# Two mixture-of-experts routers and a unit norm run inside the layer norm's block, the picking of routed tokens takes eight highest at a time, and an expert's bias is added on VectorE

## The chip, the cores and the metric

The kernel runs as one program on one core of a Trainium2 chip. The metric is the device time of one execution in microseconds. All data are fp32. An fp32 product of two 128x128 tiles, or a transpose of one, shows in the trace as one or two matmul instructions on TensorE (PE), each with a weight load (PEld) of its own: a transpose or a product with a 0/1 matrix takes one, a product of two full fp32 tiles two.

## The reference

Eight blocks run one after the other on x, 4096 tokens (16 rows of 256) by 128, each as `x = layernorm(x + block(x))`. Four of them matter here.

- **L0's FFN** is a mixture of 8 experts. `logits = x @ router_w + router_b`; the two highest of each token get the softmax of the two as their gates; the output is the gated sum of the two experts.
- **L1's FFN** is a mixture of 8 experts with bias. The scores are `softmax(x @ gate_w.T + gate_b)`; of the two highest of a token only the expert with the higher number is used (as the kernel computes it, `win`), with its score as the gate. Its output is `gelu(xs @ w1 + b1) @ w2 + b2` of the scaled token `xs`.
- **L2's FFN** has a light attention over all tokens and a heavy one over routed tokens:

```
def rmsnorm(x, gamma):
    norm = jnp.maximum(jnp.linalg.norm(x, axis=-1, keepdims=True), 1e-12)
    return x / norm * x.shape[-1] ** 0.5 * gamma
def route(x, routing_token, num_tokens):
    s = jnp.einsum('bnd,d->bn', x, routing_token)
    scores = coor_descent(s, k)                        # 50 iterations
    sel_scores, sel_idx = jax.lax.top_k(scores, num_tokens)
    return (sel_scores + stop_gradient(1.0 - sel_scores), sel_idx)
...
light_out = light_local_attn(x, gamma_light, wq_light, wkv_light, wo_light)
scores_q, idx_q = route(x, q_routing_token, NQ)        # 128 of the 256 of a row
scores_kv, idx_kv = route(x, kv_routing_token, NKV)    # all 256
heavy_out = zeros.at[b, idx_q].set(heavy_attn(...) * scores_q)
return light_out + heavy_out
```

- **Every layer norm** is applied at the start of the next block: a block ends with x + block(x) in `X` and each token's mean and variance in `core.mv`.

## The kernel before

`X` holds the tokens, 32 tiles of 128 tokens (partitions) by 128; `XT` holds them transposed, 128 by 4096. A group is 4 tiles, 512 tokens, and fills one of the 8 PSUM banks. The program is a row of Blocks. Within one, each engine runs its own instructions in the order in which they are written, and waits on semaphores; no scheduler moves anything. Between two Blocks all engines meet at a barrier, and SyncE (SP) then gives each new semaphore one credit, for which the first instructions wait.

**normalize_stage** (L296, L313, L323, L302). VectorE (DVE) makes 1/std and writes the 32 normalized tiles, PE transposes 8 groups of 4 into 8 banks, ScalarE (ACT) copies groups 0 to 4 to `XT`, and DVE, done with its own, groups 5 to 7.

**gate_stage** (L1412 to L1447), a Block of its own behind a norm, in two places (names g_...). PE forms the logits with the router's weights as the stationary operand, 8 rows by 512 tokens at a time; ACT copies them to `g_LT`; 32 small transposes (L1416) turn them by token. DVE adds the bias, and for each of the 32 tiles takes MAX8 and FIND_INDEX8 (L1454, L1458). L0 then turns the gates back by expert with 32 transposes (L1427) and 8 copies by ACT to `f_gatesT`, which the FFN's Block stores to DRAM (L1555) and loads spread over the partitions (L1561, `f_spread`); DVE multiplies by it at L1628. L1 has a third Block, **l1_places** (names p_..., L1740 to L1776), that counts the tokens of each expert before each token (`f_place`) and the expert of each of the 40 sorted tiles (`f_expert`).

**l1_ffn.** POOL scatters the 32 tiles of tokens to `x_sorted` (L1872), SP loads them back in order of expert (L1857, `f_xin`), and a loop written out over 40 sorted tiles (slots) follows. In a slot PE transposes the scaled tile n (L1899), forms the hidden rows of n-1 (L1906) and the output of n-2 (first the bias as a row of ones by `f_b`, L1914, then four products, L1917). DVE scales tile n (L1972), and adds, normalizes and takes the moments of older tiles (L1975 to L1990). POOL copies the next expert's `w1` to `f_w` and scatters finished tiles. PE, ACT and POOL each read the number of the expert into a register (L1839).

**l2_ffn.** normalize_stage; routing_start (the scores of the two routing tokens, 16 matmuls of 32 rows, and the scaling of six weights by gamma on DVE); normalize_stage once more as unit norm (names nu_...; squares and sums on DVE, then `normed`, L294); the light attention, `wide_stage` "5l", in which the 50 iterations of the descent are interleaved; routing_finish (L3316 to L3368), which ranks each token among the 256 of its row by comparing it with all of them, two rows at a time; the heavy attention, "5h", which takes the tokens whose rank is below 128, in the order of their rank.

Of the kernel before, what the change touches and what calls it, by code (L numbers as in the profile page):

```python
# [23 lines left out]
ALU = mybir.AluOpType  # L24
# [13 lines left out]
W_COLS = (5760, 8864)  # L38
# [29 lines left out]
def shape_constants():  # L68
# [16 lines left out]
    before = np.concatenate([(c < q), (c < q + P)], 1).astype(np.float32)  # L85
# [10 lines left out]
        ("bucket", onehot), ("future", neg), ("logk", logk), ("before", before),  # L96
        ("order", np.tile(np.arange(P, dtype=np.float32), (P, 1))),
        ("iota8", np.tile(np.arange(8, dtype=np.float32), (P, 1))),
    ]
# [12 lines left out]
STAGED = {"rope32q": 0, "ones": 0, "rope32k": 0, "rope8q": 2, "rope8k": 2, "bucket": 2, "future": 2, "before": 5, "order": 5}  # L112
# [26 lines left out]
def place_weights(items, region_cols):  # L139

    at, out = 0, {}
    for name, rows, cols in items:
# [15 lines left out]
        ("l1_lower", 128, 128), ("l1_ones", 128, 128), ("l1_multiples", 128, 32), ("l1_earlier", 128, 64),  # L158
# [3 lines left out]
        ("l2_tok", 128, 64), ("before", 128, 512), ("order", 128, 128),  # L162
# [66 lines left out]
def normalize_stage(core, ctx, n, first=False, unit=None, into=None, beside=None, next_weights=()):  # L229
# [5 lines left out]
    SQUARES = 8  # L235
    LOADS = 4 if first else 0
    BY_ACT = 5
    credited = []
    sem = lambda s: new_sem(core, ctx, f"n{n}_{s}", credited)
    with ExitStack() as mem:  # L240
        mem.callback(retire, core, credited)
        std = mem.enter_context(nc.sbuf_tensor(f"n{n}_std", [P, TILES], F32))
        sq = mem.enter_context(nc.sbuf_tensor(f"n{n}_sq", [P, SQUARES, DM], F32)) if unit is not None else None
        normed = X if unit is None and into is None else unit if into is None else into
        x_loaded = [sem(f"x_loaded{k}") for k in range(LOADS)]
        var_ready, std_ready, rstd_ready = sem("var_ready"), sem("std_ready"), sem("rstd_ready")
        group_normed, group_turned, squared = sem("group_normed"), sem("group_turned"), sem("squared")
        ident = core.const("ident")
        block = mem.enter_context(nc.Block())

        @block.sync
        def _(sp):
# [9 lines left out]
            if beside:  # L262
                beside(sp)

        @block.vector
        def _(dve):
# [3 lines left out]
            elif unit is not None:  # L270
                squared_so_far = counter(CREDIT)
                for c in range(0, TILES, SQUARES):
                    dve.tensor_tensor(sq[:, :, :], X[:, c:c + SQUARES, :], X[:, c:c + SQUARES, :], ALU.mult
                                      ).then_inc(squared, 1)
                    dve.wait_ge(squared, squared_so_far())
                    dve.tensor_reduce(core.rstd[:, c:c + SQUARES], sq[:, :, :], AX.X, ALU.add).then_inc(squared, 1)
                    dve.wait_ge(squared, squared_so_far())
# [1103 lines left out]


def gate_stage(core, ctx, n, w, m, dve_part, act_part, outs, setup=None):


    nc = core.nc
    credited = []
# [2156 lines left out]
```

## Time and profile before

| | |
|---|---|
| median of 3 runs | 2970.11 us (2969.63 to 2972.64) |
| profiled execution | 2968.71 us |
| its span | 2966.9 us |
| PE busy | 2421.8 us (82%) |
| weight loads (PEld) busy | 1869.1 us (63%) |
| DVE busy | 1951.4 us (66%) |
| ACT busy | 1396.2 us (47%) |
| POOL busy | 1397.5 us (47%) |
| mean granted TensorE clock | 0.932 of full |

The span runs from the first to the last instruction of the profiled execution; 1.8 us of its time lie outside. The shares are means over a program whose stages have different limits, so a stretch has to be read by itself. The granted clock is 1.0 at 2.4 GHz and 0.50 at 1.2 GHz.

### The profile page before, as it was taken

The numbers are of one execution on the slowest core, as the hardware profiler recorded it, in microseconds if no ns is written. First come the engines' busy times: TensorE is split into PE (matmuls) and PEld (weight loads), VectorE is DVE, ScalarE is ACT, GpSimd is POOL, SyncE is SP. The second block draws the span as 40 slices with busy tenths as digits, with TensorE's granted clock in tenths as the row PEclk, the third lists the DMA queues.
The fourth block names the chain that finished last, engine by engine and source line by source line (L and its number), as shares of the span: only waits on it lengthen the run. The fifth ranks groups of instructions, "written<-read, shape, count | busy, mean of one in ns | idle before, by whom it ended". The sixth has DMA issues, their size and how long they took to land. (4 is left out here: it accounts for less than half of the span.)

```text
span 2966.9 us, 73365 instructions
## 1 busy us (share of the span) xinstructions
PE 2421.8 (82%) x21662; PEld 1869.1 (63%) x21662; DVE 1951.4 (66%) x8496; ACT 1396.2 (47%) x3314; POOL 1397.5 (47%) x1606
## 2 busy tenths in 40 slices
PE   5888888779588872778998778956897899999977
PEld 4666666536366650666777567745776777777755
DVE  3666666646488873337888679975555676777746
ACT  1333333322366651445666446623554666656624
POOL 2666666400266652547777345632331444455401
PEclk7999999989799995889999989978999999999978
DMA  2000000022200001130000100000000000000001
GB/s 68 2 1 0 0 0 0 19 59 57 90 2 0 0 24 41 52 94 2 0 0 0 37 1 1 0 0 1 2 0 21 2 1 0 0 0 0 0 1 29
DMA packets 38235, 45.06 MB, mean 15 GB/s; under 512 B 6265, under 2 KB 28658, under 8 KB 37750
## 3 DMA queue, kind: packets, MB, share of 16 engines
q1 hardware_dynamic: 35774, 38.43, 4.6%
q0 software_dynamic: 2304, 4.79, 0.5%
q8 instruction: 68, 1.11, 0.2%
q14 instruction: 89, 0.73, 0.1%
HBM read 36.17 MB, written 9.74 MB: 15 GB/s over the span
## 5 line engine op out<-in xcount | busy, mean ns | idle before, releaser
L1081 POOL TENSOR_TENSOR a_sm<-a_sm,a_top 128x512 f32<-128x512 f32 x512 | 523.4, 1040 | 308.0 <-DVE a_top L879 306.0
L1004 ACT ACTIVATE a_pr<-a_sm 128x512 f32<-128x512 f32 x512 | 315.1, 626 | 236.5 <-POOL a_sm L1081 132.5
L879 DVE CUSTOM_DVE_ANT_0 a_sm<-bank,cst 128x256 f32<-128x256 f32 (+1 forms) x1024 | 300.9, 352 | 120.0 <-PE bank L741 120.0
L755 PE MATMUL bank<-cst,a_pr 128*128 128x128 f32 x2304 | 307.2, 277 | 0.6 <-ACT a_pt L1014 0.5
L2921 POOL TENSOR_TENSOR a_pr<-a_sm,a_rden 128x512 f32<-128x512 f32 x192 | 197.1, 1047 | 225.9 <-DVE a_rden L2707 225.4
L755 PEld LDWEIGHTS bank<-cst,a_pr 128*128 128x128 f32 x2304 | 259.6, 142 | 27.8 <-issue 20.4
L887 DVE COPY a_pt<-bank 128x512 f32<-128x512 f32 x272 | 187.0, 688 | 129.4 <-PE bank L755 125.0
L1014 ACT ACTIVATE a_pt<-bank 128x512 f32<-128x512 f32 x304 | 177.1, 588 | 98.2 <-PE bank L755 94.3
L2681 DVE CUSTOM_DVE_ANT_0 a_sm<-bank,cst 128x256 f32<-128x256 f32 (+1 forms) x512 | 149.7, 353 | 51.0 <-PE bank L2568 43.5
L775 PEld LDWEIGHTS bank<-a_pt,a_v 128*32 128x32 f32 x4608 | 118.3, 110 | 88.6 <-issue 77.8
L879 DVE CUSTOM_DVE_ANT_0 a_sm<-bank,a_bias 128x256 f32<-128x256 f32 (+1 forms) x512 | 148.4, 353 | 33.0 <-PE bank L741 30.0
L775 PE MATMUL bank<-a_pt,a_v 128*32 128x128 f32 x4608 | 155.9, 276 | 7.4 <-DVE a_pt L887 3.8
L2997 PE MATMUL bank<-a_xs,W 128*128 128x256 f32 x544 | 140.2, 392 | 17.8 <-ACT a_q L3010 10.7
L2921 POOL TENSOR_TENSOR a5h_pr<-a5h_sm,a5h_rden 128x512 f32<-128x512 f32 x64 | 65.6, 1046 | 158.3 <-DVE a5h_rden L2707 158.3
L1071 POOL COPY a_xs<-XT 128x256 f32 (+1 forms) x54 | 21.4, 399 | 225.7 <-SPq L619 225.7
L2827 ACT ACTIVATE a_sm<-a_sm,a_top 128x256 f32<-128x256 f32 x256 | 127.1, 505 | 0.0
L879 DVE DVE_READ_ACCUMULATOR2_ANT a_top<- 128x1 f32 x1536 | 126.9, 83 | 0.0
L2997 PEld LDWEIGHTS bank<-a_xs,W 128*128 128x128 f32 x544 | 95.8, 192 | 41.3 <-ACT a_q L3010 17.6
L741 PE MATMUL bank<-a_kx,a_q 32*128 32x512 f32 (+1 forms) x896 | 111.2, 579 | 9.0 <-POOL a_kx L1162 4.6
L1019 ACT ACTIVATE a_osb<-bank 128x256 f32<-128x256 f32 (+1 forms) x96 | 43.7, 455 | 158.9 <-PE bank L775 158.9
L2568 PE MATMUL bank<-a_k,a_q 64*128 64x256 f32 (+1 forms) x1024 | 96.8, 333 | 17.7 <-ACT a_k L3010 9.3
L805 PE MATMUL bank<-cst,a_rx 128*128 128x128 f32 x256 | 48.2, 290 | 76.6 <-DVE a_top L879 74.3
(484 smaller groups left out, 6156.6 us busy)
## 6 DMA issues: line engine op xcount, KB each, us to landing
f_spread<-gate_rows SPq DMA_DIRECT2D x16, 512.0 KB, 6.8
W<-in_l_w SPq DMA_DIRECT2D x2, 2048.0 KB, 9.7
x_sorted<-in_l_blank SPq DMA_DIRECT2D x4, 660.0 KB
f_xin<-x_sorted SPq DMA_DIRECT2D x10, 264.0 KB, 2.9
X<-in_x SPq DMA_DIRECT2D x4, 512.0 KB, 6.8
a_bias<-bias_rows SPq DMA_DIRECT2D x1, 2048.0 KB, 7.9
X<-y_rows SPq DMA_DIRECT2D x8, 256.0 KB, 5.5
out_x<-X SPq DMA_DIRECT2D x8, 256.0 KB, 2.3
```

Of the source, the lines that this page charges most:

```text
L741: mm = pe.matmul(sbank[j][:, col:col + m * kw], B["q"][b][r0:r0 + rows, c, qt * P:(qt + 1) * P], B["kx"][b][r0:r0 + rows, x:x + m, 0:kw], ...
L755: mm = pe.transpose(tbank[j % 2][:, c * P:(c + 1) * P], pr[j][:, c * P:(c + 1) * P], ident)
L775: mm = pe.matmul(O[32 * group:32 * group + 32, blk * P:(blk + 1) * P], B["v"][b][:, kb, hd.slot[h], :], pt[j][:, col:col + P], start=(kb = ...
L879: ins = dve.tensor_tensor_reduce(sm[j][:, m * kw:(m + 1) * kw], sbank[j][:, m * kw:(m + 1) * kw], mk, 1.0, 3.0e38, ALU.add, ALU.min, top[: ...
L887: dve.tensor_copy(pt[j][:, :], tbank[j % 2][:, :]).then_inc(S[f"turned_out{j}"], 1)
L1004: act.activation(pr[j][:, :], sm[j][:, :], ACT.Exp, scale=-1.0).then_inc(S["probs"], 1)
L1014: act.activation(pt[j][:, :], tbank[j % 2][:, :], ACT.Copy).then_inc(S[f"turned_out{j}"], 1)
L1081: pool.tensor_tensor(whole, whole, top[:, qt, a:a + m].unsqueeze(2).to_broadcast([P, m, kw]), ALU.subtract).then_inc(S["shifted"], 1)
L2681: ins = dve.tensor_tensor_reduce(sm[s % 2 * 4 + j][:, m * kw:(m + 1) * kw], sbank[j][:, m * kw:(m + 1) * kw], mk, 1.0, 3.0e38, ALU.add, AL ...
L2827: ins = act.activation(part, part, ACT.Exp, bias=top[:, s % 2, j, m:m + 1], scale=-1.0, accum_out=den[:, s % 2, j, m:m + 1])
L2921: pool.tensor_tensor(pr[j][:, :].rearrange("p (h k) -> p h k", k=kw), sm[q % 2 * 4 + j][:, :].rearrange("p (h k) -> p h k", k=kw), rden[:, ...
L2997: mm = pe.matmul(bank[:, c * SEQ:(c + 1) * SEQ], w[:, a:a + P], xs[:, :], start=True, stop=True)
```

## The change

**Norm and routers.** normalize_stage loses its unit form and takes `follow`, an object with a part for each engine that runs in the same Block. ACT now copies all 8 groups in every normalize_stage (before 5). With `follow`, PE forms the logits by token, with a tile of `XT` as the stationary operand and the router's 8 columns as the moving one. L0Gates and L1Gates replace gate_stage, top_entries and l1_places. They hold everything as 8 experts by 32 tiles (256 elements a partition); a reduction over experts reads elements 32 apart (`by_token`). The two highest are found by a maximum, a comparison, a product with 8..1 to take the first of equals, and another maximum. The sums before a tile come from one scan. The gates of L0 leave as two 128x128 transposes; their store is issued in this Block, and the spread loads wait for the first to land before the second is issued. In L1 POOL issues the 32 scatters in this Block.

```
+            def logits(g):
+                pe.wait_ge(copied, g + 1 + CREDIT)
+                for t in range(g * G, g * G + G):
+                    mm = pe.matmul(core.bank[0][:, 8 * t:8 * t + 8], XT[:, t * P:(t + 1) * P], follow.w, start=True, stop=True)
             for g in range(GROUPS):
...
                 for t in range(G):
                     mm = pe.transpose(core.bank[g][:, t * P:(t + 1) * P], normed[:, g * G + t, 0:DM], ident)
+                if follow and g >= 2:
+                    logits(g - 2)
...
+    def first_at(self, dve, values, highest, out):
...
+        self.then(dve, dve.tensor_tensor(self.eq[:, :, :], values[:, :, :], over(highest[:, :], SHE, 1), ALU.is_equal))
+        self.then(dve, dve.tensor_tensor(self.eq[:, :, :], self.eq[:, :, :], over(self.core.const("down8"), SHE, 2), ALU.mult))
+        self.then(dve, dve.tensor_reduce(self.c[:, :], by_token(self.eq), AX.X, ALU.max))
+        self.then(dve, dve.tensor_tensor(out[:, :, :], self.eq[:, :, :], over(self.c[:, :], SHE, 1), ALU.is_equal))
...
+    def dve(self, dve):
+        dve.wait_ge(self.logits_mm, 1 + CREDIT)
+        self.then(dve, dve.tensor_tensor(self.lg[:, :, :], self.logits, over(self.b, SHE, 2), ALU.add))
+        self.then(dve, dve.tensor_reduce(self.m[:, :], by_token(self.lg), AX.X, ALU.max))
+        self.first_at(dve, self.lg, self.m, self.one)
+        self.then(dve, dve.scalar_tensor_tensor(self.rest[:, :, :], self.one[:, :, :], -BIG, self.lg[:, :, :], ALU.mult, ALU.add))
+        self.then(dve, dve.tensor_reduce(self.r[:, :], by_token(self.rest), AX.X, ALU.max))
+        dve.tensor_tensor(self.a[:, :], self.r[:, :], self.m[:, :], ALU.subtract).then_inc(self.to_exp, 1)
+        self.first_at(dve, self.rest, self.r, self.two)
...
```

On PE, in the Block of the norm that stands before L0's FFN and the Block after it, before the change:

```order
L313 MATMUL bank<-cst,X 128x128 x32
L240 UNCONDITIONAL_BRANCH
L1407 UNCONDITIONAL_BRANCH
L1412 MATMUL bank<-XT,W 8x512 x8
L1416 MATMUL bank<-cst,g_LT 128x8 x32
L1427 MATMUL bank<-cst,f_gates 8x128 x32
L1393 UNCONDITIONAL_BRANCH
```

and after it, in one Block, where L309 is the transpose and L299 the router's product by token:

```order
L309 MATMUL bank<-cst,X 128x128 x12
L299 MATMUL bank<-W,XT 128x8 x4
L309 MATMUL bank<-cst,X 128x128 x4
L299 MATMUL bank<-W,XT 128x8 x4
L309 MATMUL bank<-cst,X 128x128 x4
...
L299 MATMUL bank<-W,XT 128x8 x12
L1479 MATMUL bank<-cst,n_gates 128x128 x2
L239 UNCONDITIONAL_BRANCH
```

The products now stand between the transposes, one group of 4 behind each from the third, and the last three groups of 4 behind the last transpose; the 64 small transposes are 2 large ones.

**Bias of an expert.** `f_b` becomes 128x1024, loaded from 4 KB of DRAM to all partitions (512 KB), and DVE waits for it before its first tile. DVE adds it.

```
-                        pe.matmul(y, w("l1_ones")[0:1, :], b2[:, bass.ds(e * DM, DM)], start=True, stop=False)
...
+                    for n in behind(3):
+                        e = expert(dve, n)
+                        dve.wait_ge(down, n + 1 + CREDIT)
+                        dve.tensor_tensor(yb[n % 2][:, :], YB[n % 2][:, 0:DM], b2[:, bass.ds(e * DM, DM)], ALU.add
+                                          ).then_inc(biased, 1)
```

On DVE, in the last slot of the ramp, where the first reciprocal stands, before:

```order
L1972 TENSOR_SCALAR f_xg<-f_xin 128x128
L1975 RECIPROCAL f_rstd<-f_std 128x1
L1978 TENSOR_TENSOR f_z<-bank,f_xin 128x128
L1984 TENSOR_SCALAR f_yout<-f_z,f_mv,f_rstd 128x128
L1988 BN_STATS f_stat<-f_z 128x6
L1990 BN_AGGR f_mv<-f_stat 128x2
```

and after (L1777 reads the expert's number into a register):

```order
L1903 TENSOR_SCALAR f_xg<-f_xin 128x128
L1777 TENSOR_LOAD f_expert
L1777 ISA x2
L1907 ISA
L1907 TENSOR_TENSOR f_yb<-bank,f_b 128x128
L1911 RECIPROCAL f_rstd<-f_std 128x1
L1914 TENSOR_TENSOR f_z<-f_yb,f_xin 128x128
```

The read of the bank moved ahead of the reciprocal, with a register load ahead of it; PE waits for this read instead of for L1978.

**Unit norm.** normalize 5, routing_start and the unit norm become one Block. The unit-length tile is written from the raw `X` as (X - mean)·scale, where scale comes from the variance that is already there; `X` itself is not normalized, and the light attention's end adds unit·length. PE transposes and forms the two routing products by tile, as in a router, ACT copies the even groups (after scaling three light weights) and DVE the odd ones.

**Picking.** routing_finish loses its loop; all 32 rows of 256 scores are handled at once:

```
+            for k in range(PICKS):
+                here = sc if k == 0 else left[(k - 1) % 2]
+                dve.max(eight[k % 2][:, :], here[:, :]).then_inc(found, 1)
+                dve.wait_ge(found, k + 1 + CREDIT)
+                dve.match_replace(left[k % 2][:, :], eight[k % 2][:, :], here[:, :], -1.0).then_inc(taken, 1)
+                dve.wait_ge(taken, k + 1 + CREDIT)
```

A scan over the tokens that were replaced gives each its place; two transposes bring it by token. The heavy weights are scaled here by ACT. On DVE, one iteration's first and last operations before:

```order
L3344 ISA r_prod,r_own<-bank,cst 128x128
L3344 ISA r_own 128x1
L3351 SCALAR_TENSOR_TENSOR r_tie<-bank,r_own,W 128x256 x4
L3357 SCALAR_TENSOR_TENSOR r_ahead<-bank,r_own,r_tie 128x256 x4
L3363 ISA
L3363 TENSOR_REDUCE rank<-r_ahead 128x2
```

and the whole of the picking's end after, behind 14 more pairs like the first two rows:

```order
L3351 MAX r_eight<-r_left 32x8
L3353 MATCH_REPLACE r_left<-r_eight,r_left 32x256
L3355 TENSOR_SCALAR r_picked<-r_left 32x256
L3358 SCALAR_TENSOR_TENSOR r_place<-r_ones,r_picked 32x256
L3360 SCALAR_TENSOR_TENSOR r_row<-r_place,r_picked 32x256
L3362 TENSOR_SCALAR rank<-bank 128x32
L3366 TENSOR_SCALAR r_chosen<-rank 128x32
L3369 TENSOR_TENSOR SQ<-SQ,r_chosen 128x32
```

A chain that handled 2 of 16 rows in each of 8 iterations is a chain of 16 pairs over all rows, each waiting for the one ahead.

## Rows read from the trace of the kernel before

**Rows 1.** Busy time by stretch: us, PE, PEld, DVE, ACT, POOL, clock, DMA, GB/s

```profile
27.00:50.00 23.00, 15.29 (x64) 14.25 (x64) 10.74 (x48) 1.28 (x1) 6.21 (x18) 0.50 0.00 0
1206.50:1210.00 3.50, 3.50 (x16) 3.05 (x15) 0.00 (x0) 2.45 (x9) 1.23 (x2) 0.50 0.00 0
1214.00:1300.00 86.00, 85.83 (x653) 77.44 (x652) 40.10 (x211) 55.63 (x206) 53.58 (x68) 1.00 0.17 48
```

**Rows 2.** Timeline, first router: start, us, engine, line, output<-inputs, [idle before <-releaser]

```profile
581.74 4.67 PE L313 MATMUL bank<-cst,X 128*128 128x128 f32 x20 [5.44 <-DVE X L296]
582.68 0.71 PEld L313 LDWEIGHTS bank<-cst,X 128*128 128x128 f32 x4 [0.25 <-DVE X L296]
585.75 0.42 PEld L313 LDWEIGHTS bank<-cst,X 128*128 128x128 f32 x4 [0.31 <-DVE X L296]
...
613.53 0.42 DVE L1516 TENSOR_TENSOR g_two<-g_two,g_p 128x256 f32<-128x256 f32 x1
613.99 0.42 DVE L1518 TENSOR_TENSOR f_gates<-g_one,g_two 128x256 f32<-128x256 f32 x1
...
622.73 0.36 SPq L1555 DMA_DIRECT2D gate_rows<-f_gatesT  x1
...
635.93 0.69 DVE L1628 TENSOR_TENSOR f_hid<-f_prod,f_spread 128x512 f32<-128x512 f32 x1 [6.93 <-DMA f_spread<-gate_rows]
```

**Rows 3.** Timeline of weight loads in the first attention's stage

```profile
33.49 1.78 PEld L478 LDWEIGHTS bank<-W,kv_xs 128*128 128x128 f32 x8 [0.92 <-DVE KV L489]
```

**Rows 4.** Single lines: ns min/median/max, first and last start, forms

```profile
L276 DVE TENSOR_REDUCE rstd<-nu_sq x4: 1219/1220/1220, 1703.7 to 1711.3; 128x8 f32<-128x1024 f32 x4
L2324 DVE TENSOR_REDUCE f_S<-f_ec x1: 1873/1873/1873, 2915.3 to 2915.3; 128x128 f32<-128x1024 f32 x1
L1454 DVE MAX8 g_vals<-g_lg x32: 150/151/170, 604.0 to 606.1; 128x8 f32<-128x8 f32 x32
```

**Rows 5.** Timeline, second router and the scatter by expert

```profile
1109.12 5.84 PE L313 MATMUL bank<-cst,f_moved 128*128 128x128 f32 x24 [5.44 <-DVE f_moved L296]
...
1158.65 1.17 POOL L1872 DMA_INDIRECT x_sorted<-f_moved,f_place  x1 [12.85 <-SPq L204]
...
1198.00 0.96 POOL L1872 DMA_INDIRECT x_sorted<-f_moved,f_place  x1 [0.31 <-issue]
...
1203.22 0.29 DVE L1972 TENSOR_SCALAR f_xg<-f_xin 128x128 f32<-128x128 f32 x1 [44.73 <-DMA f_xin<-x_sorted]
```

**Rows 6.** The page: DMA issues, KB each, median us from issue to landing

```profile
f_xin<-x_sorted SPq DMA_DIRECT2D x10, 264.0 KB, 2.9
X<-in_x SPq DMA_DIRECT2D x4, 512.0 KB, 6.8
```

**Rows 7.** Timeline of one slot of the expert loop

```profile
1228.69 0.48 PE L1914 MATMUL bank<-f_b,W 1*128 x2
...
1229.11 0.97 PEld L1917 LDWEIGHTS bank<-W,f_hT 128*128 128x128 f32 x8
...
1230.26 0.16 DVE L1975 RECIPROCAL f_rstd<-f_std 128x1 f32<-128x1 f32 x1 [1.31 <-ACT f_std L1953]
...
1231.20 0.48 PE L1914 MATMUL bank<-f_b,W 1*128 x2
```

**Rows 8.** The register load of an expert's number on ACT

```profile
L1839 ACTq TENSOR_LOAD <-f_expert x40: 272/278/491, 1204.4 to 1304.5; - x40
```

**Rows 9.** Timeline, start of L2's FFN and of its light attention

```profile
1683.32 5.70 PE L313 MATMUL bank<-cst,X 128*128 128x128 f32 x24 [5.44 <-DVE X L296]
...
1719.87 1.88 DVE L302 COPY XT<-bank 128x512 f32<-128x512 f32 x3
...
1724.51 0.74 POOL L2904 COPY a5l_xs<-XT 128x256 f32<-128x256 f32 x2 [49.33 <-SPq L2448]
```

**Rows 10.** Timeline of the picking

```profile
1965.91 0.41 ACT L3316 ACTIVATE r_sc<-d_t 32x256 f32<-32x256 f32 x1 [4.60 <-DVE d_t L3327]
...
2019.05 0.19 DVE L3368 TENSOR_TENSOR SQ<-SQ,r_chosen 128x32 f32<-128x32 f32 x1
```

## What the change is forecast to do

> **What bounds the kernel now.** The page gives PE 82% of the span, but the change touches stretches in which PE does little or nothing, so I read the busy time by stretch first. In the steady part of the expert loop PE is busy for 85.83 of 86 us at full clock [rows 1]: there an operation taken from PE shortens the slot, until another engine needs as long. Before it DVE waited 44.73 us for the scattered tiles [rows 5], while POOL scatters and nothing else has anything to do. Then the timelines. Around each router one operation hands to the next: 54.2 us lie between the first transpose (581.74) and the first product with the spread gates (635.93), which waited 6.93 us for a transfer [rows 2]; 49.5 us between the transpose at 1109.12 and the first scatter at 1158.65 [rows 5]. Before the light attention 41.2 us pass from the first transpose, at 1683.32, to 1724.51, when POOL begins its first copy [rows 9]. The picking holds PE and POOL up from the exponential at 1965.91 to 2019.24 (2019.05 + 0.19) [rows 10]. In these four stretches everything is on the path, so each microsecond counts whole.
>
> **Two prices that all of them need.** A DVE operation on 128x256 with a wait for the one before starts 0.46 us after it (613.53 to 613.99, of which 0.42 is the operation) [rows 2]. A maximum or sum over strided elements costs more: 1024 contiguous elements took 1.220 us, 1024 strided ones 1.873 [rows 4], 0.64 ns an element, 0.16 us for 256. The second price is TensorE's. Four transposes of a group load for 0.71 us at half clock and 0.42 at full [rows 2]. The four router products of a group are full fp32 products with a tile as the stationary operand, 8 weight loads; such 8 loads took 1.78 us at half clock [rows 3] and 0.97 at full [rows 7].
>
> **Norm with router.** DVE delivers a group each 1.03 us, and PE turns the first three as now, until 2.7 us after its start t. Then 5 groups of transposes and 8 of products are due: 5·0.71 + 8·1.78 = 17.8 us at half clock, 5·0.42 + 8·0.97 = 9.9 at full. PE becomes what this block waits for, and the granted clock decides. Now the clock rises 4.0 us after t in the first norm (581.74 to 585.75) [rows 2]. But in the attention's stage of 27 to 50 us the clock stays 0.50 with PE busy 15.29 of 23 us, and in the expert loop, PE busy throughout, it is still 0.50 at 1206.5 to 1210 and full by 1214 [rows 1], 3.3 to 10.8 us behind the first tile at 1203.22 [rows 5]. Between 4.0 and 10.8 I take the middle, 7.4. By then 4.7 us of the 17.8 are done; the rest at full clock takes 9.9·(1 - 4.7/17.8) = 7.3, and the logits stand at t + 14.7. The bounds are t + 13.2 (rise at 4.0) and t + 20.5 (no rise).
>
> **A, L0's router.** t = 581.74, logits at 596.4. DVE then runs 15 steps of 256 elements at 0.46 us, four of them strided at 0.16 more, and five small ones, the wait for ACT among them, some 1.1 us: 8.7. Two transposes and one copy of 128x256 on ACT take about 1.2. So the store is issued at 606.3 rather than 622.73. Store and load took 13.2 us (to 635.93) [rows 2]; the four loads then shared the queue. Now the first pair goes alone: a store of some 3 us, and 6.8, what a transfer of 512 KB needs to land [rows 6], 10.0 with the wait. The barrier, 1.4 us before, is hidden behind it. First gated product at 616.4 instead of 635.93: **19.5 us**.
>
> **B, L1's router.** t = 1109.12, logits at 1123.8. Up to `placed` DVE has some 31 steps of about 256 elements, 9 strided, and small ones between, with two waits (exponential, counts): 18.9 us, most of it 30·0.46 + 9·0.16 = 15.2 and the rest at small prices. POOL, in the same block, scatters at 1142.9 instead of 1158.65, no barrier standing between: 15.8 less. The 32 scatters keep their pace of (1198.00 - 1158.65)/31 = 1.27 us [rows 5]. Behind them something is given back. Now 4.3 us pass from the last scatter's end (1198.96) to the first tile at 1203.22. The barrier now lies behind the scatters (2.3 us with the credit), and SP's first transfer there is the spread `f_b`, 512 KB, for which DVE waits before its first tile, with the read of the scattered tiles behind it on the queue. I take 5.5 us for both, between 2.9 (the tiles alone, 264 KB) and the 6.8 of 512 KB [rows 6]. 2.3 + 0.4 + 5.5 = 8.2 against 4.3, 3.9 back: 15.8 - 3.9 = **11.9 us**.
>
> **C, bias on DVE.** PE's slot is 2.51 us (1228.69 to 1231.20). From L1914 to the first load of L1917 are 0.42 us [rows 7]; without it, 40 slots save 40·0.41 = **16.4 us**, to a slot of 2.09. The lower bound is the operation's own least share, 0.25 us a slot: 10. Does another engine need more? DVE is busy 40.10 us in 34.4 slots [rows 1], 1.17 a slot; the new addition (0.27) and the register load make it 1.9. The load takes 0.28 us where ACT does it [rows 8], with some 0.17 of register work. ACT: 55.63/34.4 = 1.62, and its own load 0.45: 2.07, the same as PE's, so it is full too. DVE now waits 1.31 us for ACT in each slot [rows 7]; the load falls into that wait. But `biased` comes later than the product ends by 0.6, and the next `f_xg` behind it by 1.2, and PE wants it 2.09 behind: 0.3 to spare. The Trainium skill (DMA: Bandwidth & Descriptors, Latency and other measured facts) puts a floor of about 600 ns on a register load, by which ACT's slot would be 2.39 and the gain some 5 us in place of 16.4. The trace has 0.28 and decides.
>
> **D, unit norm's block.** Before the first tile DVE and ACT have one more root, product, maximum, reciprocal and product, 1.3 us: t = 1683.32 + 1.3 = 1684.6, logits at 1699.4, of the same shape as a router's. Product with the length, two transposes, copy and maximum add 1.6: 1701.0. The work that stands there now ends at 1719.87 + 1.88 = 1721.75 [rows 9]; the way on to POOL's copy stays: **20.8 us**. Squares, sums (4·1.22 [rows 4]), the second norm and two barriers are gone. The scaling of weights goes to ACT, ahead of its first copy, 3·0.6 us beside DVE's first groups; if it delays the first copies, PE has transposes to do.
>
> **E, picking.** No instruction of the trace reads 256 elements in MAX8; with 8 it took 0.15 [rows 4]. At a sum's 1.05 ns an element, 248 more make 0.41. The replacement is two instructions, a load of 8 (0.09) and a pass like any of 256 elements, 0.42. With two waits a pair takes 1.00 us. It could be 0.8 if the two overlap, or 2.0 if each pass takes twice the time. 16 pairs are 16.0 us, and the tail (mark, scan, product, two transposes, three short steps) 2.5. The exponential ends 0.4 us sooner, at 1965.9, since the memsets are POOL's. So 1984.4 against 2019.24: **34.8 us** [rows 10]. The roots `sel`, the weights' scaling and the memsets run on POOL and ACT beside it, 3 us in all under 16.
>
> **F, the copies.** In the norms 2, 6 and 7 the last three copies, 1.88 us on DVE [rows 9], are ACT's now and end 0.4 us sooner each: **1.1 us**.
>
> **Sum.** 19.5 + 11.9 + 16.4 + 20.8 + 34.8 + 1.1 = 104.5. The profiled execution took 2968.71 us, so 2864.2; the median of the runs, 1.4 above it, gives 2865.6, rounded 2865.
>
> **Weighed against the skill.** The row says that strided reduction costs 0.64 ns more an element; 13 such reductions in A and B are 2.1 us, already in the sum. The Trainium skill (Advanced Engine Details and Errata, SBUF Cachelines) speaks against this layout, elements 32 apart in fp32: each access on another line of 16 bytes pays a penalty. The trace agrees and gives the penalty a size that the pages leave out.
>
> **The rivals.**
> - *The clock never rises in the three blocks.* For it speaks the stage of 27 to 50 us [rows 1], in which PE works with gaps; against it that with a backlog PE has no gaps here. Three times 20.5 - 14.7 = 5.8: 17.4 us less, 2883.
> - *The expert loop doesn't follow PE.* DVE's chain behind `down` has 0.3 us to spare, ACT's sum is level with PE's. If the slot stays at 2.51, 16.4 are lost: 2882. At 2.3, half.
> - *Picking at 2.0 us a pair*: 16 us less, 2881. Nothing in the rows speaks for it but the absence of such an instruction.
> - *Slower.* The register load on DVE: each slot it stands ahead of the read of the bank, and PE, ACT and POOL wait behind that. The other terms give 88.1 us; spread on 40 slots, 2.2 us. The kernel is slower by 6 us from a slot of 2.51 + 94/40 = 4.86, which needs a load of 3.4 us where ACT's takes 0.28. At a load of 3.5, the slot is 4.96 and the time 2970 - 88 + 98 = 2980.
> - *The change does not do what it says*: the longest of the stretches stays because another transfer ends it. For L0 the bound is the store and load, which I count in full; in the others no transfer stands at the end [rows 9, 10].
>
> **How the numbers follow.** I give my forecast 0.70, no rise of the clock 0.12, the loop 0.08, the picking 0.06, slower 0.02, no change 0.02. Downwards the clock's rise at 4.0 us gives 4.5, `f_b` with the tiles in 2.9 us gives 2.6, pairs of 0.8 us 3.2: together 10, and 5 for prices taken too high: 2850. Upwards each of the three rivals alone ends at 2881 to 2883; two at once and the last two cases are left out. So 2850 to 2884. Faster by over 0.2% (6 us, about what a measurement of this kernel tells from no change) holds in all cases but the last two: 0.97; within it 0.01; slower 0.02.
>
> **What would show it.** In the profile of the changed kernel: logits of the first router ended 14.7 us behind the first transpose, with eight loads at 0.97 in the second half of that time; the store at 606; the first scatter at 1142.9 and the first tile 8.2 us behind the last scatter's end; a slot of 2.09 with PE still busy all of it; POOL's copy into the light attention 19.1 us behind the block's first transpose (now 41.2); 16 pairs of 1.00 us. The sum is wrong if PE idles in the slot, if loads stay at 1.78 in the blocks, or if a pair of the picking shows over 1.2 us.

## The result, and the profile after

The changed kernel takes 2898.11 us (median of 4 runs, 2896.35 to 2898.73). The kernel before took 2971.32 beside it (4 runs, 2969.63 to 2972.64). The ratio is 0.9756, 95% interval 0.9744 to 0.9767: 73 us less, where 105 were forecast, and the time lies above the range's 2884. A correction: the section on the reference says that L1's experts use a gelu; they use a relu. No number rests on it.

| profiled execution | before | after |
|---|---|---|
| its time | 2968.71 us | 2898.5 us |
| its span | 2966.9 us | 2896.7 us |
| PE / DVE busy | 2421.8 / 1951.4 us | 2390.4 / 1916.4 us |
| ACT / POOL busy | 1396.2 / 1397.5 us | 1391.7 / 1391.9 us |
| mean granted clock | 0.932 | 0.932 |

The sums of busy time moved by 31 and 35 us for the two large engines and by 5 for the others, and say little; the stretches say it. Between the same two instructions of each stage:

| term | from, to | before | after | gain | forecast |
|---|---|---|---|---|---|
| A, L0's router | end of the attention before, to the first gated product | 58.5 | 46.0 | 12.5 | 19.5 |
| B, L1's router | first transpose to first tile | 94.1 | 90.6 | 3.5 | 11.9 |
| C, expert loop | first tile to L2's attention | 129.9 | 119.4 | 10.5 | 16.4 |
| D, unit norm | first DVE step of the norm to POOL's copy | 44.1 | 29.6 | 14.5 | 20.8 |
| E, picking | exponential to the last mark | 53.3 | 18.4 | 35.0 | 34.8 |

Together 76.0. The span fell by 70.2; the other 5.8 went the wrong way outside these five stretches, most of it in stages whose instructions the change does not touch (below).

The first router in the timeline of the changed kernel (start, us, engine, line; L309 is the transpose, L299 the router's product), against [rows 2]:

```profile
583.15 3.08 PE L309 MATMUL bank<-cst,X 128*128 128x128 f32 x12 [5.45 <-DVE X L282]
...
585.81 1.83 PEld L299 LDWEIGHTS bank<-W,XT 128*128 128x128 f32 x8
...
598.08 5.24 PEld L299 LDWEIGHTS bank<-W,XT 128*128 128x128 f32 x24
...
603.53 0.42 DVE L1492 TENSOR_TENSOR n_lg<-bank,W 128x256 f32<-128x256 f32 x1 [13.35 <-PE bank L299]
603.99 0.58 DVE L1493 TENSOR_REDUCE n_m<-n_lg 128x32 f32<-128x256 f32 x1
...
613.14 0.39 SPq L1470 DMA_DIRECT2D gate_rows<-n_turned_rows  x1
...
624.83 0.69 DVE L1709 TENSOR_TENSOR f_hid<-f_prod,f_spread 128x512 f32<-128x512 f32 x1 [3.22 <-DMA f_spread<-gate_rows]
```

The logits stand 20.4 us behind the first transpose, the bound that the prediction gives for no rise of the clock (20.5), and the last loads are still at the slow price, 5.24 us for 24. The same stretch and the steady loop by windows (us, then PE, PEld, DVE, ACT and POOL busy, granted clock, DMA share, GB/s):

```profile
583.10:603.40 20.30, 20.25 (x96) 19.64 (x96) 7.08 (x28) 4.78 (x8) 0.00 (x0) 0.50 0.21 61
1095.10:1115.40 20.30, 20.21 (x96) 19.64 (x96) 7.12 (x28) 4.78 (x8) 0.00 (x0) 0.50 0.43 153
1200.00:1260.00 60.00, 55.88 (x447) 50.94 (x446) 48.51 (x189) 40.69 (x156) 41.98 (x53) 1.00 0.22 63
```

PE worked for 20.25 of 20.30 us at a clock of 0.50, in both routers. In the loop PE is no longer full, 56 of 60 us, where it was 85.83 of 86 [rows 1], and DVE is busy for 48.5 of 60. The second router and what follows it, against [rows 5]:

```profile
1115.56 0.42 DVE L1562 TENSOR_TENSOR n_lg<-bank,W 128x256 f32<-128x256 f32 x1 [13.34 <-PE bank L299]
...
1134.08 0.18 DVE L1598 CAST f_place<-n_placef 128x32 uint32<-128x32 f32 x1
...
1135.17 1.17 POOL L1554 DMA_INDIRECT x_sorted<-f_moved,f_place  x1 [42.00 <-DVE f_place L1598]
...
1174.60 0.96 POOL L1554 DMA_INDIRECT x_sorted<-f_moved,f_place  x1 [0.30 <-issue]
...
1180.64 0.34 SPq L1789 DMA_DIRECT2D f_b<-in_l_b  x1
...
1185.79 0.28 DVE L1903 TENSOR_SCALAR f_xg<-f_xin 128x128 f32<-128x128 f32 x1 [5.09 <-DMA f_xin<-x_sorted]
```

From the last scatter's end (1175.56) 5.1 us pass until SP's first instruction of the next Block and 5.15 more to the first tile: 10.2, where 4.3 stood before and 8.2 were forecast.

The unit norm's block, against [rows 9] (L3194 the transpose, L3203 the routing products, L2840 POOL's copy):

```profile
1656.40 0.40 DVE L3245 TENSOR_SCALAR rstd<-mv 128x32 f32<-128x32 f32 x1 [1.73 <-SPq L205]
...
1661.26 3.07 PE L3194 MATMUL bank<-cst,unit 128*128 128x128 f32 x12 [7.94 <-DVE unit L3264]
...
1681.55 0.27 DVE L3271 TENSOR_TENSOR rs_by_token<-bank,length 128x64 f32<-128x64 f32 x1 [4.22 <-PE bank L3203]
...
1685.96 0.74 POOL L2840 COPY a5l_xs<-XT 128x256 f32<-128x256 f32 x2 [29.20 <-SPq L2384]
```

Here the products move only 2 columns (the two routing tokens), and they too are there 20.3 us behind the first transpose (forecast 14.7). POOL's copy stands 24.7 us behind it, where 19.1 were named.

One slot of the loop on DVE and POOL, against [rows 7] (L1907 adds the bias, L1914 the token, L1814 copies an expert's weights):

```profile
1198.72 0.25 DVE L1903 TENSOR_SCALAR f_xg<-f_xin 128x128 f32<-128x128 f32 x1
...
1199.37 0.29 DVE L1907 TENSOR_TENSOR f_yb<-bank,f_b 128x128 f32<-128x128 f32 x1 [0.40 <-issue]
...
1199.65 0.62 POOL L1814 COPY f_w<-W 128x512 f32 x1
1199.70 0.73 DVE L1914 TENSOR_TENSOR f_z<-f_yb,f_xin 128x128 f32<-128x128 f32 x1
...
1201.02 0.25 DVE L1903 TENSOR_SCALAR f_xg<-f_xin 128x128 f32<-128x128 f32 x1
...
1201.33 0.33 PE L1830 MATMUL bank<-cst,f_xg 128*128 128x128 f32 x1 [0.15 <-DVE f_xg L1903]
```

PE waits for `f_xg` (0.15 us here), and L1914 takes 0.73 us, where L1907, an addition of the same shape with a bank as an operand, takes 0.29. Over the whole loop DVE idles ahead of L1907 for 21.2 us, half of it before its own uncounted instructions, among them the register load (busy us, mean ns | idle before, and what ended it):

```profile
L1914 DVE TENSOR_TENSOR f_z<-f_yb,f_xin 128x128 f32<-128x128 f32 x39 | 24.4, 625 | 0.1
...
L1907 DVE TENSOR_TENSOR f_yb<-bank,f_b 128x128 f32<-128x128 f32 x39 | 11.4, 292 | 21.2 <-issue 10.9 <-PE bank L1847 10.3
```

The picking (E), of which the second of the 16 pairs and the end stand here, against [rows 10]:

```profile
1928.59 0.41 ACT L3334 ACTIVATE r_sc<-d_t 32x256 f32<-32x256 f32 x1 [3.64 <-DVE d_t L3347]
...
1929.99 0.42 DVE L3351 MAX8 r_eight<-r_left 32x8 f32<-32x256 f32 x1
...
1930.44 0.08 DVE L3353 MATCH_VALUE_LOAD r_left<-r_eight,r_left 32x8 f32 x1
1930.52 0.40 DVE L3353 MATCH_REPLACE8 r_left<-r_eight,r_left 32x256 f32<-32x256 f32 x1
...
1946.76 0.19 DVE L3369 TENSOR_TENSOR SQ<-SQ,r_chosen 128x32 f32<-128x32 f32 x1
```

Three questions follow: why the clock stayed down with PE full, what fills DVE in the slot, and what stands behind the scatters.

### The profile page after: what moved, and what is told of

Its sections match the earlier page's. It is cut to its first block and busy times, and to the rows that moved or that the text cites. A ratio compares the mean times of both kernels' runs of the same rounds, so it can differ in the third digit from the quotient of the medians.

```text
span 2896.7 us, 72685 instructions
## 1 busy us (share of the span) xinstructions
PE 2390.4 (83%) x21556; PEld 1872.2 (65%) x21556; DVE 1916.4 (66%) x8183; ACT 1391.7 (48%) x3310; POOL 1391.9 (48%) x1598
## 5 line engine op out<-in xcount | busy, mean ns | idle before, releaser
L2933 PE MATMUL bank<-a_xs,W 128*128 128x256 f32 x544 | 142.3, 397 | 16.9 <-ACT a_q L2946 10.8
```

The lines of the kernel that those rows point to most:

```text
L2933: mm = pe.matmul(bank[:, c * SEQ:(c + 1) * SEQ], w[:, a:a + P], xs[:, :], start=True, stop=True)
```

## The experiments

All are edits of the changed kernel, except one of the kernel before. Ratios are to the kernel before; the changed kernel's is 0.9756.

**Why the clock stays down: how much a product moves, or where it stands.** The router's product moves 8 columns against 8 weight loads. The first edit moves 128 columns in both routers (those beyond the router's 8 are other weights, whose products nobody reads) into the bank that the transposes have left, and DVE adds the bias in 8 pieces:

```
-  mm = pe.matmul(core.bank[0][:, 8 * t:8 * t + 8], XT[:, t * P:(t + 1) * P], follow.w, ...)
+  mm = pe.matmul(core.bank[g][:, (t % G) * P:(t % G + 1) * P], XT[:, t * P:(t + 1) * P],
+                 core.W[follow.stage % 2][:, 0:P], ...)
```

> Question: why did the granted clock stay at 0.50 through the two router blocks although PE is recorded busy for 20.2 of 20.3 us? The router's product moves 128 columns instead of 8 (the router's own 8 and 120 of the weights beside them, which are thrown away), and DVE adds the bias in 8 pieces. The 8 weight loads per group stay. Theory columns: with 8 columns a product PE counts as busy in the profile but gives the clock little to rise on; with 128 the clock rises within the block, loads fall from 1.83 to about 0.97 us per group, each router block's logits end 3 to 6 us sooner, the pieces give 1 us back, so 4 to 10 us faster in all than the changed kernel (2898), about 2891. Rival idle-before: the clock depends on what PE did before the block, not on columns; then it stays at 0.50, the moving columns cost PE up to 0.4 us a group, and the kernel is 1 to 8 us slower.

Measured: 2885.85 us (2882.7 to 2889.01), ratio 0.9712 (0.9696 to 0.9729), 12 us faster than the changed kernel though PE moves 16 times as much. In the stretches of the table A takes 38.2 us (46.0) and B 84.4 (90.6), 14 us less together. Windows of the first router, columns as above, and two rows of its timeline:

```profile
582.20:585.20 3.00, 2.99 (x13) 2.44 (x14) 3.00 (x13) 1.19 (x2) 0.00 (x0) 0.50 0.56 160
586.00:594.70 8.70, 8.70 (x79) 8.54 (x77) 3.24 (x13) 2.99 (x5) 0.00 (x0) 1.00 0.16 50
```

```profile
586.46 0.97 PEld L299 LDWEIGHTS bank<-W,XT 128*128 128x128 f32 x8
...
594.85 0.87 DVE L1450 TENSOR_TENSOR n_lg<-bank,W 128x32 f32<-128x32 f32 x8 [5.61 <-PE bank L299]
```

The first transpose starts at 582.21. By 586.0 the clock is full, the loads of the same products fall to 0.97, and the logits stand at t + 12.6, in the second router at t + 13.7: about the best case of the prediction, t + 13.2.

The second edit keeps the 8 columns and puts all products behind the last transpose:

```
-                if follow and g >= 2:
-                    logits(g - 2)
             if follow:
-                for g in range(GROUPS - 2, GROUPS):
+                for g in range(GROUPS):
```

> The same question from the other side: all products by token stand behind the last transpose, in both routers and in the unit norm's block; nothing else changes. In the norms without a router the clock rises about 4 us behind the first transpose. Theory columns: the clock rises there too, at full clock 8 groups take 7.8 us; if it holds, the logits end at t + 16.5 instead of t + 20.4, 3.9 us sooner in each of three blocks, about 11 us faster, 2887. If products of few columns let it fall again, the later groups show 1.83 us loads and the gain is 0 to 5 us. Rival idle-before: no rise at all, the backlog becomes longer by what overlapped: 3 us slower in each block, about 2907.

Measured: 2898.73 us (2893.6 to 2902.62), ratio 0.9752 (0.9735 to 0.9769), no different from the changed kernel. The first router tells why: the transposes bring the clock up (the last four load in 0.42 us), the products, from 588.3 on, run at 1.00 for 2 us more and then lose it. The products of the three blocks are there at t + 19.5, 17.2 and 22.9, where the changed kernel has 20.4, 20.4 and 20.3.

```profile
587.78 0.42 PEld L309 LDWEIGHTS bank<-cst,X 128*128 128x128 f32 x4 [0.55 <-DVE X L282]
```

```profile
588.20:590.20 2.00, 2.00 (x21) 2.00 (x20) 0.00 (x0) 0.60 (x1) 0.00 (x0) 1.00 0.00 0
591.00:599.80 8.80, 8.80 (x43) 8.80 (x42) 0.00 (x0) 0.00 (x0) 0.00 (x0) 0.50 0.00 0
```

The third is the control: banks and the 8 pieces on DVE as in the first edit, but 8 columns in each product.

```
-                 core.W[follow.stage % 2][:, 0:P], ...)
+                 follow.w, ...)      # into 8 columns of bank[g]
```

> The control for the 128 columns: the router's products write to the same places in eight banks and DVE adds the bias in the same eight pieces, but each product moves its own 8 columns only. Theory columns: the clock stays at 0.50 through both blocks as in the changed kernel, 8 loads take 1.83 us, the pieces cost 0.5 us a block, 2899. Rival layout: the spread over banks was what let the clock rise (or shortened the chain); then it is near the 2886 of the kernel with 128 columns.

Measured: 2900.59 us (2896.54 to 2902.95), ratio 0.9762 (0.9746 to 0.9779): the gain of the first edit is gone. In the first router:

```profile
583.60:586.60 3.00, 3.00 (x30) 3.00 (x29) 3.00 (x13) 1.38 (x3) 0.00 (x0) 0.97 0.70 229
587.20:600.60 13.40, 10.63 (x52) 10.54 (x51) 3.01 (x14) 1.79 (x3) 0.00 (x0) 0.50 0.00 1
```

In the first router the clock was up from about 583.8, 3.1 us behind the first transpose, and fell again by 587.2 among the products of 8 columns, and the logits stand at t + 17.3; in the second its loads stayed at 1.83 us throughout, and they stand at t + 20.4. Between this run and the first edit only the columns differ. With 8 the clock does not stay up in any layout or place that was tried; with 128 it does. Why it rose for a while in the one router and not in the other these runs do not show. No size between 8 and 128 was tried.

**What fills the slot.** First the bias goes back to PE, C alone undone:

```
+  pe.matmul(y, w("l1_ones")[0:1, :], b2[:, bass.ds(e * DM, DM)], start=True, stop=False)
...
-  dve.tensor_tensor(yb[n % 2][:, :], YB[n % 2][:, 0:DM], b2[:, bass.ds(e * DM, DM)], ALU.add
-                    ).then_inc(biased, 1)
```

> The expert's bias goes back to PE (row of ones by the bias of the expert, 4 KB load), everything else as in the changed kernel. It prices the bias edit alone. The slot should return from 2.30 to 2.50 us: 40 x 0.20 = 8 us longer in the loop; the gap from the last scatter to the first tile should shrink, since the 512 KB load is gone, from 10.2 us to 7 to 9. Sum: 5 to 8 us slower than 2898, about 2904. If the bias edit had gained what was forecast on a path that something else now ends, the kernel would be within 3 us of 2898.

Measured: 2903.24 us (2886.07 to 2904.86), ratio 0.9748 (0.9716 to 0.978), the slot 2.46 us. The runs are too wide apart to size it by the whole; by the slot the change's bias is worth 0.18 us, 7 us in 40 slots.

Then the bias stays on DVE but is added in place, in PSUM, so that L1914 has only one operand in SBUF. PE now waits for L1914, as before the change:

```
-  dve.tensor_tensor(yb[n % 2][:, :], YB[n % 2][:, 0:DM], b2[...], ALU.add)
+  dve.tensor_tensor(YB[n % 2][:, 0:DM], YB[n % 2][:, 0:DM], b2[...], ALU.add)
...
-  dve.tensor_tensor(z[n % 4][:, :], yb[n % 2][:, :], xin...
+  dve.tensor_tensor(z[n % 4][:, :], YB[n % 2][:, 0:DM], xin...
```

> DVE adds the bias in place in PSUM and then adds f_xin from there, so the second addition has one operand in SBUF instead of two; PE waits for the second addition again. Same number of operations. Theory shared port: the second addition shows 0.72 us instead of 0.29 because both operands are in SBUF and POOL copies f_w at that moment; with an operand in PSUM it takes 0.27 to 0.29, the slot falls from 2.30 to PE's 2.09 (DVE's own sum is then 1.87), 8 us faster, about 2890. Rival register load: the slot is held by the register load ahead of the read of the bank (0.41 us before f_yb in which DVE waits for nothing else), the addition waits only because it has time; the slot stays at 2.2 to 2.30 and the time within 3 us of 2898.

Measured: 2885.95 us (2884.22 to 2887.66), ratio 0.971 (0.9693 to 0.9726), 12 us faster than the changed kernel. A slot takes (1262.2 - 1182.0)/39 = 2.06 us by the first and last start of `f_xg`, and PE is nearly full again, 59 of 60 us:

```profile
L1903 DVE TENSOR_SCALAR f_xg<-f_xin x40: 253/270/286, 1182.0 to 1262.2; 128x128 f32<-128x128 f32 x40
```

```profile
1195.00:1255.00 60.00, 58.98 (x498) 56.92 (x499) 44.67 (x216) 44.42 (x179) 47.43 (x59) 1.00 0.23 66
```

```profile
1200.62 0.62 POOL L1814 COPY f_w<-W 128x512 f32 x1
1200.84 0.27 DVE L1914 TENSOR_TENSOR f_z<-bank,f_xin 128x128 f32<-128x128 f32 x1
```

The addition begins in the midst of POOL's copy and takes 0.27 us. Of the 12 us the slots give (2.28 - 2.06)·40 = 8.8. The first tile already starts 3.8 us sooner than in the changed kernel (1181.95 against 1185.79), ahead of all that the edit touches, so the rest is not the edit's. In the next one the operands stay in SBUF and POOL copies a single column of the next expert's `w1` from the fourth slot on, so it leaves out most of the copy, and most experts then work with an older matrix:

```
-  pool.tensor_copy(w1[n % 3][:, :], w("l1_w1")[:, bass.ds(e * BANK, BANK)]).then_inc(w1_copied, 1)
+  cols = BANK if n < 3 else 1
+  pool.tensor_copy(w1[n % 3][:, 0:cols], w("l1_w1")[:, bass.ds(e * BANK, cols)]).then_inc(w1_copied, 1)
```

> In the changed kernel POOL copies only the first column of the next expert's w1 from the fourth slot on (so from there on most experts work with an older matrix; DVE's own work is the same). It asks who DVE's second addition waits for in the slot. Theory shared port: the addition with both operands in SBUF takes 0.72 us because POOL's copy of 0.62 us runs at that moment; without it 0.29, and the slot falls from 2.30 to about 2.0, as it did with the operand in PSUM: 12 us faster, 2886. Rival PSUM: reading an operand from SBUF that was just written costs the 0.43 us whatever POOL does; then the addition stays at 0.72 and the time at 2898.

Measured: 2887.86 us (2876.24 to 2889.4), ratio 0.9712 (0.9692 to 0.9732), slot 2.04 us. The durations of the later addition (ns, min/median/max) in the changed kernel and then in this one:

```profile
L1914 DVE TENSOR_TENSOR f_z<-f_yb,f_xin x40: 273/715/728, 1192.4 to 1281.4; 128x128 f32<-128x128 f32 x40
```

```profile
L1915 DVE TENSOR_TENSOR f_z<-f_yb,f_xin x40: 271/272/294, 1189.0 to 1268.6; 128x128 f32<-128x128 f32 x40
```

Same operation, same operands: 0.715 us beside the copy and 0.272 without it, in the medians. The last of this group doubles the register load on DVE:

```
+                        expert(dve, n)
                         e = expert(dve, n)
```

> DVE reads the expert's number into a register twice in each slot; all else as in the changed kernel. Theory: the slot of 2.30 us is DVE's own sum, and the load is part of it (0.41 us ahead of f_yb, 26 times of 40 with nothing else awaited): the second load adds 0.4 to 0.45 us a slot, 16 to 18 us slower, 2915. Rival: the load falls into a wait for PE or ACT; then at most 3 us slower.

Measured: 2904.33 us (2900.52 to 2906.95), ratio 0.9773 (0.9758 to 0.9788), slot 2.49 us. This fits neither size that was expected: a second load costs 0.21 us a slot. Two things happen at once.

```profile
L1915 DVE TENSOR_TENSOR f_z<-f_yb,f_xin x40: 272/291/293, 1189.9 to 1288.7; 128x128 f32<-128x128 f32 x40
```

```profile
1220.00 0.29 DVE L1908 TENSOR_TENSOR f_yb<-bank,f_b 128x128 f32<-128x128 f32 x1 [1.04 <-issue]
```

The idle time ahead of the bias ("issue") grows from 0.40 to 1.04 us, and in turn the later addition no longer meets POOL's copy: 0.64 more, 0.42 back. So the load stands on DVE's path, and not, where the prediction put it, in a wait for ACT.

**What stands behind the scatters.** First POOL's scatters go back to the Block of the loop, so that the barrier is passed before them and `f_b` comes during them. The edit moves the loop over `pool.indirect_dma_start(x_sorted...)` and its two waits from the router's part for POOL to the head of the loop's.

> The 32 scatters go back from the router's block to the expert loop's block, as in the kernel before; all else as in the changed kernel. There 10.2 us pass from the last scatter's end to the first tile (5.1 of them before the loop's block shows its first instruction, 5.1 for the bias and the tiles), where 8.2 were forecast. Theory barrier: a barrier behind outstanding scatters costs 5.1 us, one behind DVE's work some 2.3; with the scatters behind it both the barrier's excess and the 512 KB load are hidden, the first scatter starts 1.2 us later (2.3 instead of 1.1 behind the place's cast), the gap behind the last one is again 4.3: 10.2 - 4.3 - 1.3 = 4.6 us faster than 2898, about 2893.5. Rival: the tiles' read needs its 5 us in any case and the barrier's 5.1 us moves ahead of the scatters; then no change within 2 us.

Measured: 2896.12 us (2892.96 to 2897.12), ratio 0.9745 (0.9729 to 0.9761), 2 us less in the medians and within the intervals, less than expected.

```profile
1136.37 1.17 POOL L1804 DMA_INDIRECT x_sorted<-f_moved,f_place  x1 [45.06 <-SPq L205]
...
1175.71 0.95 POOL L1804 DMA_INDIRECT x_sorted<-f_moved,f_place  x1 [0.30 <-issue]
...
1181.13 0.28 DVE L1902 TENSOR_SCALAR f_xg<-f_xin 128x128 f32<-128x128 f32 x1 [44.92 <-DMA f_xin<-x_sorted]
```

From the last scatter's end to the first tile 4.5 us pass in place of 10.2, but the first scatter starts 4.15 us behind the cast that makes `f_place` (at 1132.22), in place of 1.09 (1134.08 to 1135.17): 5.7 back, 3.1 lost.

Then only the load of `f_b` moves, into the router's Block:

```
+            sp.dma_start(b2[:, :], core.dram["l1_b2"].to_broadcast([P, 8 * DM])).then_inc(b2_in, 16)
```

> The load of the spread bias (512 KB) is issued in the router's block, ahead of the blank rows, instead of at the start of the loop's block; all else as in the changed kernel. Theory load: of the 5.1 us from the block's first instruction to the first tile the kernel before needed 2.9 (issue of the tiles at 1200.29 to 1203.22), so the bias load ahead on the queue costs about 2.0: 2 us faster, 2896. Rival: the tiles' own read is what is waited for, 0 us.

Measured: 2896.69 us (2893.61 to 2897.95), ratio 0.9746 (0.973 to 0.9763).

```profile
1178.84 1.49 SPq L1795 DMA_DIRECT2D f_xin<-x_sorted  x3
...
1181.90 0.29 DVE L1903 TENSOR_SCALAR f_xg<-f_xin 128x128 f32<-128x128 f32 x1 [3.01 <-DMA f_xin<-x_sorted]
```

3.06 us from the Block's first transfer to the first tile, 5.15 with the 512 KB of `f_b` ahead of it (and 3.2 in the run with the bias on PE, whose load is 4 KB): the load is worth 2.1 us in the trace. The whole is 1.4 us less than the changed kernel's, within its interval. The gap ahead of the Block is 5.3.

**The picking alone**, in the kernel before: its `routing_finish` is replaced by that of the change, nothing else.

> The picking alone, put into the kernel before (the weights of the heavy attention stay scaled where they were). The trace of the changed kernel shows 35.0 us from exponential to chosen scores less than before. If the parts add up, this kernel is 35 us faster than the kernel before: ratio 0.988. If the light attention or the heavy one behind it gave part of it back for reasons of their own, 30 or less.

Measured: 2936.34 us (2934.67 to 2938.9), ratio 0.9883 (0.9867 to 0.99): 35 us, as in the trace.

**Together.** 128 columns in all three blocks and the addition in PSUM:

> Products of 128 columns in all three blocks (routers and unit norm; the surplus columns are thrown away) and the bias added in place in PSUM. The first alone in the two routers gave 12 us, the second alone 12. The unit norm's block has the same shape: its logits should end about 7 us sooner, less 0.6 for eight small reads instead of one. If they add: 12 + 12 + 6 = 30, 2868. If the clock's rise in one block is bought with a fall in the next stretch, less.

Measured: 2871.86 us (2869.35 to 2875.25), ratio 0.9668 (0.9651 to 0.9684). The routing products stand at t + 13.0 in the unit norm's block (20.3 in the changed kernel). The whole is some 4 us above the 2868 that was expected of the sum, less than its interval is wide. With the scatters' edit as well:

> The parts that gained, together: products of 128 columns in the three blocks, the bias added in place in PSUM, and the scatters in the loop's block. 2871.9 was measured for the first two, the last gave 2.0 alone: 2870, ratio to the kernel before 0.966. If the barrier's saving needs the slower logits to hide it, 2872.

Measured: 2869.43 us (5 runs, 2865.93 to 2870.92), ratio 0.9662 (0.9648 to 0.9675), mean granted clock 0.942, slot 2.05 us. It beats both kernels, by the ratios 28 us below the changed one; against the version without the scatters' edit the intervals overlap.

## Why the prediction was wrong in size

**The clock, in A, B and D.** The step that failed is "Between 4.0 and 10.8 I take the middle, 7.4", and with it the ground for giving its rival 0.12: "with a backlog PE has no gaps here". PE had none, and the clock stayed at 0.50. The logits came at t + 20.4, 20.4 and 20.3 instead of 14.7, together 17.0 us, what the rival gives as 17.4. The three edits show that it goes with the columns that a product moves (8 in the routers, 2 in the unit norm's block). The loads of [rows 3], 1.78 us for 8, belong to the stage of 27 to 50 us, in which PE stayed at half clock with gaps; I read the gaps as its cause and had no row in which PE was full at products of 8 columns.

**The loop, in C.** The step that failed is "1.9" for DVE's need in a slot, and the "0.3 to spare" that hang on it. The slot came to 2.28 us (0.24 less, where 0.42 were forecast). DVE's operations of a slot are those that were named, but the later addition takes 0.72 us instead of 0.27, because with the bias in `f_yb` both its operands lie in SBUF and POOL's copy of 0.62 us runs beside it. Before the change the operand was a bank (L1978), so no row showed the meeting; with the operand in PSUM or the copy cut to one column the slot is 2.06 or 2.04, a little below the 2.09 forecast. The Trainium skill has the rule (SBUF — State Buffer, SBUF: two separate sides): VectorE and GpSimd share a pair of ports as an exclusive lock, which an operation of VectorE with two inputs in SBUF takes against one of GpSimd that reads SBUF, and the later of the two is blocked. The trace agrees, 0.715 against 0.272 us, and the rule was not weighed. The register load (0.28 us on ACT [rows 8]) was put in a wait for ACT that did not last: DVE idles 10.9 us over the loop with nothing else awaited, and a second load adds 0.64 us of such idle time in a slot.

**Behind the scatters, in B.** "3.9 back" became 6.0. The transfers were sized rightly (5.15 us for 5.5); the barrier was not, 5.1 us in place of 2.3 + 0.4. The barrier of the same place takes 2.6 us when the scatters stand behind it, so the excess goes with a barrier that follows 32 of them. What in it waits was not isolated.

**Store and load, in A.** 10.0 us became 11.7, 1.9 for the store and 9.8 for the load of the first pair, against the 6.8 of [rows 6]. No run took this apart.

**What held.** The chain on DVE: 8.4 us in L0's router (8.7 forecast) and 18.7 in L1's (18.9); the strided maximum costs 0.58 where a contiguous operation costs 0.42, the 0.16 that [rows 4] gives. The picking: a pair takes 0.96 us (1.00), the term 35.0 (34.8), and alone in the kernel before 35.2. The way from logits to POOL's copy in D: 4.4 us, as forecast; only its first transpose came 0.7 us later than forecast. F lies outside the five stretches: in the norms 2, 6 and 7 the last copy into `XT` ends 8.38 us behind the first transpose where it ended at 8.83, 1.35 us in all (1.1 forecast). But in the first norm of the program, which the prediction left out, it ends 0.6 us later (8.52 for 7.89).

**The sum.** 104.5 forecast, 76.0 measured in the stages: of the 28.5 between, 17.0 are the clock, 5.9 the loop's stage, 2.1 behind the scatters, 1.7 store and load, and 1.1 is F, which the table does not hold; what is left is under 1 in all. The further 5.8 us, by which the rest of the span grew, are a sum of several. The first norm's 0.6 is in it. The light attention, from POOL's first copy to the exponential, took 241.4 us before and 242.6 after; its last step, which the change gave a product with the length, takes 0.35 us in place of 0.29 for each of the 32 tiles, and the prediction has no term for it (241.4 and 240.7 with the old step, 242.5 to 244.0 in all runs with the new one). From DVE's first instruction to its last, L2's attention took 348.2 us before and 351.9 after, L1's 325.9 and 323.7; all behind the picking took 947.7 and 949.8. None of the kernels here edits the two attentions, and they took 348.2 to 354.0 and 322.4 to 325.9; behind the picking it was 947.5 to 953.1. So these parts move by as much as is to be explained. A cause in the change is not excluded, since the two kernels with the old norm have the shortest L2 attention, 348.2 and 349.1, and all others 349.8 or more; it stays open.

**The range.** It left out the case that happened, several rivals in part at once ("two at once ... are left out"). The clock took its 17 us in all three blocks at once, from one cause, and the loop's half (8 at 2.3 a slot) stood on other grounds and came too, 5.9 in its stage. With the smaller misses this is 2864.2 + 28.5 = 2892.7, past the range's end, and 2898.5 with the 5.8 that are partly open.

## What to carry to other kernels

Where a product moves few columns, do not take the full clock for granted because TensorE will be busy: look for a row at that shape, and try moving more columns than are needed, which here saved 12 us in two routers (14 by the stretches of the trace). When an edit moves an operand of a VectorE operation from PSUM to SBUF, look what GpSimd reads at that time; keep one operand in PSUM. Before two rivals are left out together, ask whether a single cause or two independent ones can bring both, since a range of single misses is too narrow.

## What the runs showed of the hardware

- 64 matmuls of fp32 products, a full 128x128 stationary tile with 8 moving columns, and 32 transposes among them kept TensorE busy for 20.25 of 20.30 us at a granted clock of 0.50, and the clock that transposes had raised to 1.00 fell to 0.50 under such products alone (8.80 of 8.80 us busy at 0.50). With 128 columns, among the same transposes, 8.70 of 8.70 us ran at 1.00.
- A VectorE addition of 128x128 with both operands in SBUF took 0.715 us beside a GpSimd copy of 128x512, 0.272 without it, and 0.27 beside it with one operand in PSUM.
- The barrier behind 32 indirect transfers of GpSimd took 5.1 to 5.3 us; without them ahead of it 2.6 passed from the last VectorE step to the first scatter behind it.
- In 32 partitions MAX8 over 256 elements took 0.42 us, and the replacement 0.08 + 0.40.
